# The second layer's attention of a decoder kernel, written as 384 equal slots

## The reference

```python
x = x + _L1_attn_ref(_layernorm(x, axis=-1), L1_attn_W_kqv, L1_attn_b_kqv, L1_attn_W_proj, L1_attn_b_proj, L1_attn_slopes)

def _L1_attn_ref(x, W_kqv, b_kqv, W_proj, b_proj, slopes):
    B, S, E, H = (2, 512, 256, 16)
    D = E // H
    kqv = x @ W_kqv + b_kqv
    k, q, v = jnp.split(kqv, 3, axis=-1)          # each reshaped to (b, s, H, D)
    attn = jnp.einsum('bqhd,bkhd->bhqk', q, k) * (1.0 / jnp.sqrt(jnp.float32(D)))
    bias = slopes[:, None, None] * jnp.tril(rel)  # rel = j - i
    bias = jnp.where(j > i, NEG_INF, bias)
    attn = jax.nn.softmax(attn + bias[None], axis=-1)
    y = jnp.einsum('bhqk,bkhd->bqhd', attn, v).reshape(b, s, e)
    return y @ W_proj + b_proj
```

## Time and profile before

| | |
|---|---|
| runs | 2440.0, 2426.59, 2440.98 us |
| profiled execution | 2440.0 us, span 2440.0 us |
| TensorE matmul busy | 2194.9 us (90%) |
| VectorE, ScalarE, GpSimd busy | 1186.6, 961.3, 641.1 us |
| mean granted TensorE clock | 0.945 |

### The profile page before, as it was taken

How to read it: one execution, slowest core, us unless ns; L and a number is a source line. 1 busy time by engine, 2 the same in 40 slices (tenths; PEclk the granted TensorE clock), 3 DMA queues, 4 the chain that set the end, 5 groups by cost and what they waited for, 6 DMA issues and landing times. The chain is left out here.

```text
span 2440.0 us, 41800 instructions
## 1 busy us (share of the span) xinstructions
PE 2194.9 (90%) x13788; PEld 1746.8 (72%) x13789; DVE 1186.6 (49%) x3470; ACT 961.3 (39%) x1878; POOL 641.1 (26%) x821
## 2 busy tenths in 40 slices
PE   6997888779999688888889879988999999999998
PEld 4664455568999445555555457778899999999998
DVE  4553788755334456666665345535322222222245
ACT  2222455333444344444444413320255555555411
POOL 1112667744401233333332211105400000000063
PEclk9997999889999789998999889989999999999999
DMA  9930000123222424442333010054211111111033
GB/s 321 386 109 1 1 1 33 46 72 117 70 69 84 97 54 88 88 88 49 83 80 70 2 56 4 3 193 148 88 31 34 34 34 34 32 32 34 26 110 101
DMA packets 151007, 183.45 MB, mean 75 GB/s; under 512 B 25490, under 2 KB 119250, under 8 KB 150738
## 3 DMA queue, kind: packets, MB, share of 16 engines
q1 hardware_dynamic: 136962, 146.51, 21.0%
q0 software_dynamic: 12288, 33.57, 4.4%
q10 hardware_dynamic: 1616, 1.57, 0.2%
HBM read 73.34 MB, written 74.19 MB: 60 GB/s over the span
## 5 line engine op out<-in xcount | busy, mean ns | idle before, releaser
L2462 ACT ACTIVATE a_prob<-a_st_ps 128x512 f32<-128x512 f32 (+1 forms) x384 | 197.6, 523 | 302.5 <-PE a_st_ps L2341 300.3
L2539 DVE CUSTOM_DVE_ANT_0 a_s_ps<-a_s_ps,a_causal 128x512 f32<-128x512 f32 (+3 forms) x512 | 241.0, 515 | 124.2 <-PE a_s_ps L2324 123.5
L1983 PE MATMUL e_up_ps<-e_xT,e_ring 128*128 128x128 f32 x2272 | 276.7, 275 | 0.0
L1983 PEld LDWEIGHTS e_up_ps<-e_xT,e_ring 128*128 128x128 f32 x2272 | 270.7, 192 | 3.7
L1935 POOL DMA_INDIRECT e_wgu<-slots_y,slot x64 | 61.2, 957 | 620.1 <-DMA slots_y<-e_y 575.6
L2013 ACT ACTIVATE e_ring<-e_wgu 128x512 f32 (+2 forms) x355 | 180.9, 531 | 75.6 <-PE e_up_ps L1983 73.9
L2324 PE MATMUL a_s_ps<-a_ks,rf_qs 68*128 68x512 f32 (+3 forms) x512 | 155.9, 373 | 60.7 <-DVE a_most L2539 47.5
L2018 ACT ACTIVATE e_hT<-e_up_ps 128x512 f32<-128x512 f32 x103 | 61.5, 597 | 371.9 <-PE e_y_ps L1993 364.4
L2341 PE MATMUL a_st_ps<-rf_qs,a_ks 128*128 128x512 f32 (+3 forms) x512 | 186.4, 415 | 15.7 <-DMA rf_qs<-a_m_lo 12.5
L2254 POOL TENSOR_SCALAR_AFFINE_SELECT a_prob<-a_prob 128x256 f32<-128x256 f32 x256 | 101.8, 423 | 367.2 <-ACT a_prob L2462 367.0
L1993 PE MATMUL e_y_ps<-e_wd,e_hT 128*128 x852 | 195.7, 379 | 0.0
(11 more groups left out here) (465 smaller groups left out, 4021.5 us busy)
## 6 DMA issues: line engine op xcount, KB each, us to landing
slots_x<-zero_row SPq DMA_DIRECT2D x4, 8448.0 KB, 50.6
e_xin<-slots_x SPq DMA_DIRECT2D x142, 128.0 KB, 2.0
rf_qs<-late_w SPq DMA_DIRECT2D x64, 256.0 KB, 5.8
a_ks<-late_w SPq DMA_DIRECT2D x64, 256.0 KB, 6.4
slots_x<-e_y SPq DMA_DIRECT2D x71, 128.0 KB, 1.7
slots_y<-e_y SPq DMA_DIRECT2D x71, 128.0 KB, 1.7
e_wgu<-in_L_ffn_wg SPq DMA_DIRECT2D x8, 688.0 KB, 9.7
e_wgu<-in_L_ffn_wu SPq DMA_DIRECT2D x8, 688.0 KB, 10.9
```

What stands on the lines that cost most here:

```text
L1983: last = pe.matmul(up_ps[:, j, bank, (first + n) * P:(first + n + 1) * P], weights, xT[:, j, k * P:(k + 1) * P], start=k == 0, stop=k == K ...
L2462: act.activation(prob[:, gr % 2, u // 3, (u % 3) * BANK:(u % 3) * BANK + cols], st_ps[:, u % 2, 0:cols], ACT.Exp).then_inc(exp_done, 1)
L2539: last = dve.tensor_tensor_reduce(s_ps[:, u % 2, off:off + cols], s_ps[:, u % 2, off:off + cols], causal[:, S - cols:], 1.0, -3.0e38, ALU. ...
```

## The change

The stage's 8 x 48 key units become slots 0 to 383, and each engine's program is one loop over the slots. A slot has one query unit (that of `slot + LEAD`, LEAD = 18) and one key unit; 18 query units run ahead of slot 0. Everything else has a fixed slot in the group (u) or in the sequence (`at`, 0 to 47). The row scaling of the next sequence moves from VectorE (`vector_rows`) to ScalarE (`scalar_rows`, one tile a slot), with its offsets on GpSimd; statistics and combines are done a tile at a time. The values of sequence 0 are projected ahead of slot 0.

The transfers of queries and keys go by groups of four heads: `spread_group`, 8 transfers of half the size, four times a sequence, each after the exponentials of the same group of the sequence before; for groups 0 and 1 of sequence 0 the four query transfers each go out from SyncE and the four key transfers from ScalarE. For this the weights and biases are ordered by (d, h) within 64 columns, which takes 8 GpSimd instructions of half the size instead of 4, and 8 bias loads instead of 4.

```diff
-    SCORES_AT = (1, 2, 1, 2, 1, 2, 1, 2, 0, 0, 0, 0)
-    TURN_AT, OUTPUTS_AT, KEPT_AT, TURN_OUTPUTS_AT = 9, 3, 7, 11
+    SEQ = G * UNITS
+    SLOTS = B * SEQ
+    LEAD = UNITS + 6
+    OUTPUTS_AT = {3: (0,), 4: (1,), 5: (2,), 6: (3,)}
+    TURN_MAXIMA_AT, HIGH_AT, LOW_AT, KEPT_AT, TURN_OUTPUTS_AT, NORMALISE_AT = 7, 8, 8, 9, 11, 1
+    VALUES_AT, KEEP_VALUES_AT = {0: 0, 1: 1, 2: 2, 4: 3}, {7: 0, 8: 1}
+    ROWS_AT, TURN_ROWS_AT, KEEP_ROWS_AT = {1: 0, 3: 1, 4: 2, 5: 3}, 10, 10
+    QK_AT, HIGH_QK_AT, LOW_QK_AT = {12: 0, 14: 1, 34: 2, 37: 3}, {13: 0, 15: 1, 35: 2, 38: 3}, {14: 0, 16: 1, 36: 2, 39: 3}
+    TURN_HEADS_AT, KEEP_HEADS_AT, PROJECT_AT, ADD_AT = 20, 20, {22: 0, 24: 1, 26: 2, 29: 3}, {26: 0, 31: 1}
+    COMBINE_AT, STATS_AT, WHOLE_STATS_AT = {17: 0, 18: 1, 28: 2, 29: 3}, {33: 0, 34: 1, 35: 2, 37: 3}, 40
...
+        def spread_part(eng, b, gr, part, which):
+            n = gr % (P // GP) * GP
+            dst, src = ((qs, (hi, lo)[part % 2][n:n + GP, 0]), (ks, (hi, lo)[part // 2][n:n + GP, 1]))[which]
+            eng.dma_start(dst[part:PARTS:4, gr * GH:(gr + 1) * GH, :].bitcast(F32), src.bitcast(F32)).then_inc(spread[gr], 16)
...
+            def spread_group(b, gr):
+                sp.wait_ge(qk_lo, 4 * b + 2 * (gr // 2) + 2)
+                after(sp, exp_done, UNITS * (G * (b - 1) + gr + 1))
+                for part in range(4):
+                    for which in range(2):
+                        spread_part(sp, b, gr, part, which)
...
+            sp.wait_ge(qk_lo, 2)
+            for gr in range(2):
+                for part in range(4):
+                    spread_part(sp, 0, gr, part, 0)
+            place_maxima(0)
+            spread_group(0, 2)
+            spread_group(0, 3)
+            for b in range(B):
+                if b:
+                    spread_group(b, 3)
                 for gr in range(G):
+                    if G * b + gr + 1 < B * G:
+                        place_maxima(G * b + gr + 1)
+                    if b + 1 < B and gr < G - 1:
+                        spread_group(b + 1, gr)
...
+            for slot in range(SLOTS):                       # TensorE
+                n, u = slot // UNITS, slot % UNITS
+                b, at = slot // SEQ, slot % SEQ
+                if slot + LEAD < SLOTS:
+                    score_by_query(slot + LEAD)
+                if u in OUTPUTS_AT and n:
+                    for t in OUTPUTS_AT[u]:
+                        outputs(n - 1, t)
+                if u == TURN_MAXIMA_AT and n + 1 < B * G:
+                    turn_maxima(n + 1)
+                if b and at in VALUES_AT:
+                    project_v(b, VALUES_AT[at])
+                if b + 1 < B:
+                    if at == TURN_ROWS_AT:
+                        norm.tensor(b + 1, free=[(v_kept, 2 * b + 2)])
+                    if at in QK_AT:
+                        project_qk(b + 1, QK_AT[at])
...
+                if u == TURN_OUTPUTS_AT and n:
+                    turn_outputs(n - 1)
+                score_by_key(slot)
...
+            for slot in range(SLOTS):                       # ScalarE
+                exponential(slot)
+                if u == HIGH_AT and n + 1 < B * G:
+                    high_maxima(n + 1)
...
+            for slot in range(SLOTS):                       # VectorE
+                if slot + LEAD < SLOTS:
+                    maximum(slot + LEAD)
+                if u == LOW_AT and n + 1 < B * G:
+                    low_maxima(n + 1)
+                if u == NORMALISE_AT and n >= 2:
+                    normalise(n - 2)
+                if b + 1 < B and at in LOW_QK_AT:
+                    low_qk(b + 1, LOW_QK_AT[at])
```

More of the change, by code:

```diff
@@ L103, in vector_stats, with vector_tile_stats, vector_whole_stats @@
     def vector_stats(self, b):
+        self.vector_tile_stats(b, range(TB))
+        self.vector_whole_stats(b)
+    def vector_tile_stats(self, b, tiles):
         v, x, st = self.nc.vector, self.g.x, self.stats
-        for t in range(TB):
+        for t in tiles:
             v.bn_stats(st[:, t, :], x[:, b * TB + t, :]).then_inc(self.stats_done, 1)
+    def vector_whole_stats(self, b):
+        v, st = self.nc.vector, self.stats
         v.wait_ge(self.stats_done, b * TB + TB)
@@ L147, in gpsimd_offset, with scalar_rows @@
         p.tensor_tensor(self.offset[:, :], self.minus[:, :], self.rstd[:, :], ALU.mult).then_inc(self.offset_done, 1)
-    def scalar_rows(self, b, free=(), buf=0):
+    def scalar_rows(self, b, free=(), buf=0, tiles=range(TB)):
         a = self.nc.scalar
@@ L2190, in l1_attention @@
         w_done, x_done = sem("w_done"), sem("x_done")
-        spread = [sem(f"spread{i}") for i in range(KT)]
+        spread = [sem(f"spread{i}") for i in range(G)]
         m_placed = [sem(f"m_placed{i}") for i in range(G)]
@@ L2271, in _ @@
             norm.gpsimd(1)
+            norm.gpsimd_offset(1)
             pool.wait_ge(x_done, 2)
-            def body(b, nxt, following):
+            for b in range(B):
+                following = b + 2 if b + 2 < B else None
                 for gr in range(G):
@@ L2290, in body @@
                     mask(b, gr, (3,))
-                    if gr == 3 and following is not None:
-                        norm.gpsimd(following)
-            over_sequences_ahead(body)
         @block.tensor
@@ L2343, in score_by_key, with outputs @@
                 last.then_inc(st_done, 1)
[L2345 to L2346 removed]
+            def outputs(n, t):
                 if t == 0:
@@ L2435, in _ @@
+            for t in range(TB):
+                outputs(B * G - 1, t)
+            turn_outputs(B * G - 1)
             pe.wait_ge(x_done, 2 * B)
-            turn_heads(B - 1, None)
+            turn_heads(B - 1)
             for t in range(TB):
@@ L2480, in _ @@
                 high_qk(0, i)
+            act.wait_ge(qk_lo, 2)
+            for gr in range(2):
+                for part in range(4):
+                    spread_part(act, 0, gr, part, 1)
+            for i in range(2):
+                keep_values(0, i)
             act.wait_ge(front.slopes_placed, SLOPES)
@@ L2516, in _ @@
-            over_sequences_ahead(body)
-            keep_outputs(B - 1, G - 1)
+            high_maxima(0)
+            for slot in range(SLOTS):
+                n, u = slot // UNITS, slot % UNITS
+                b, at = slot // SEQ, slot % SEQ
+                exponential(slot)
+                if u == HIGH_AT and n + 1 < B * G:
+                    high_maxima(n + 1)
+                if b and at in KEEP_VALUES_AT:
+                    keep_values(b, KEEP_VALUES_AT[at])
+                if b + 1 < B:
+                    if at in ROWS_AT:
+                        norm.scalar_rows(b + 1, tiles=(ROWS_AT[at],))
+                    if at == KEEP_ROWS_AT:
+                        norm.scalar(b + 1, free=[(v_done, 2 * b + 2)])
+                    if at in HIGH_QK_AT:
+                        high_qk(b + 1, HIGH_QK_AT[at])
+                if b and at == KEEP_HEADS_AT:
+                    keep_heads(b - 1)
+                if u == KEPT_AT and n:
+                    keep_outputs(n - 1)
@@ L2543, in low_maxima @@
-            def low_maxima(b, gr):
-                n = b * G + gr
+                wait_apart(dve, s_done, s + 1, (ready, READY))
+                for t, off in Q_UNITS[u % 3]:
+                    cols = (t + 1) * P
+                    last = dve.tensor_tensor_reduce(s_ps[:, u % 2, off:off + cols], s_ps[:, u % 2, off:off + cols], causal[:, S - cols:], 1.0,
+                                                    -3.0e38, ALU.add, ALU.max, most[:, n % 2, u // 3, t:t + 1])
+                last.then_inc(max_done, 1)
```

311 lines of the change are left out of this document (111 added, 200 removed).

## The result

The kernel after took 2373.5 us (median of four, 2371.4 to 2376.5), the kernel before beside it 2439.7 us (median): a ratio of 0.975 with a 95% interval of 0.9725 to 0.9776. The forecast was 2388 us in a range of 2342 to 2430, so 52 us of saving were forecast and 66 came. The profiled execution took 2376.5 us, with a span of 2374.7.

What follows compares the result with a forecast made beforehand. TensorE was the bound in name, with 11.8 of 65.8 us a clean sequence in waits and gaps; slots -38, clock -14, start -4, SyncE +4 and front 0 sum to -52 from 2440, 2388 us, range 2342 to 2430.

Steps and rivals of the forecast that it cites:

- Slots (-38): Attention slots: equal slots cut waits and gaps from 11.8 to 7.0 us, a sequence to 61.0; -38 us over eight.
- bare slots: 17 slots a sequence without other sizeable TensorE work, where two query-unit banks allow 0.69 us, not 0.60: 1.5 us waiting.
- bulges: Slots 36 to 38, smaller at 25 and 33, where VectorE's extra work holds TensorE: 1.5 us a sequence.
- slot-8 chain: Slot 8 of each group: VectorE waits for ScalarE's split of maxima, later maxima and TensorE queue; 0.5 a group, 2.0 us.
- Rival (b): In the slots, VectorE's extra work comes in series and holds TensorE; a sequence is 65.5 us, total 2427 us; chance 0.20.
- Columns and heads: Waits in the slots for turned columns kept one slot later (0.4 us) and for heads (0.6 us), per sequence.
- Maxima and SyncE (0.2 a sequence, +4): Placed maxima leave 0.2 us of wait a sequence; SyncE's spread issues ahead of them add 4 us over the stage.
- rival (c): SyncE's queue: maxima also wait for the spread's landing, 5.8 us late twice a sequence; 93 us, total 2481; chance 0.08.
- Clock (-14): Stage slots: of 28 us lost to stretches at 1.2 GHz, half come back with fewer waits; -14 us (0 to -28).
- Start (-4): Stage lead-in: half the bytes for the first group bring the first query unit 5 us earlier, 1 goes back; -4 us.
- Front (0, at most +2.4): Ahead of attention: four more GpSimd instructions and four more bias loads on SyncE cost 0, at most 2.4 us.
- Row scaling (0): Slots 1, 3, 4, 5: ScalarE takes 4 x 0.59 us a sequence at no cost, 17 us without cover.

Runs made afterwards that it cites:

- Between the halves: Kernel after, but SyncE places the maxima of groups 2 and 0 between the two halves of the spread beside them; 2423.2 us on a slower chip, ratio 0.968.
- eight-head kernel: Kernel after with equal slots, but transfers by eight heads and four bias loads as before; 2456.5 us, ratio 1.008 to the kernel before.
- both mends: Kernel after, but SyncE alone issues the first sequence's spreads, and maxima of groups 2 and 0 stand between spread halves; 2350.3 us, ratio 0.9649 to before.

## Why the prediction was right, and where not

**Slots (-38).** The largest term, and right in its cause: the even order shortens the sequence, and putting the old distribution back brings 64.6 to 65.4 us. Forecast 61.0, measured 59.3 to 59.6. It was too narrow in naming the wait. Idle time for row maxima in the slots fell from 44.0 us before to 19.5 already in the kernel with the old distribution, whose sequences are hardly shorter, and to 10.5 with the even order; there the even order gave more by ending waits for ScalarE.

Of the waits left, VectorE's were to be 5.0 us a sequence (bare slots 1.5, bulges 1.5, the slot-8 chain 2.0). The matmuls' idle time for VectorE is 1.4, in six places of 0.20 to 0.26. Four of them are the same place in each group, the 512-column query unit of slot 9. In three of these VectorE had itself just waited for TensorE, as here:

```profile
1106.65 0.57 DVE L2547 CUSTOM_DVE_ANT_0 a_s_ps<-a_s_ps,a_causal 128x384 f32<-128x384 f32 x1 [0.23 <-PE a_s_ps L2337]
...
1107.57 0.50 PE L2337 MATMUL a_s_ps<-a_ks,rf_qs 68*128 68x512 f32 x1 [0.23 <-DVE a_most L2547]
...
1108.40 0.28 DVE L2553 SCALAR_TENSOR_TENSOR a_m_lo<-a_m_ps,a_m_hi 16x128 fp32r<-16x128 f32 x1 [0.50 <-ACT a_m_hi L2462]
```

TensorE's wait ends before VectorE turns to the split, so this is not the slot-8 chain but the two banks in bare slots: 0.7 us of the 1.4. In the fourth such place VectorE is behind a combine, and in another behind the sum, 0.46 together: its bulges, though at slots 18 and 31 and not where the forecast had them. Only the sixth, 0.21 at 1094.10, stands behind a split. VectorE waited for ScalarE's high part once in this sequence, not once a group, and 7.1 us in all slots (49.9 before). So all three terms exist, and together they are a quarter of their forecast; the slot-8 chain, the largest, was nearly nothing. Rival (b), VectorE's extra work in series at 6 us a sequence, is refuted. Columns and heads cost 0.9 instead of 1.0, outputs nothing in this sequence instead of 0.8.

**Maxima and SyncE (0.2 a sequence, +4).** The place was right, the size was not. Together they forecast 1.6 + 4 = 5.6 us of idle time; it was 12.0, nine times, at 3.0 us the worst. The 2.4 us a sequence that the forecast set against its 0.2 were waits of weight loads; by that view 18.8 us became 16.4, and by the matmuls' idle time 12.5 became 12.0. The saving of 2.2 a sequence did not come. This is SyncE's queue in one such place:

```profile
1060.66 0.57 SPq L2208 DMA_DIRECT2D rf_qs<-late_w  x1
...
1065.13 0.60 SPq L2208 DMA_DIRECT2D a_ks<-late_w  x1
1065.78 0.60 SPq L2224 DMA_DIRECT2D rf_qs<-a_m_hi  x1
1066.42 0.59 SPq L2224 DMA_DIRECT2D rf_qs<-a_m_lo  x1
```

VectorE had the low part ready at 1064.9, while SyncE was still issuing the spread until 1065.7; TensorE lost 0.70 us. Issue for issue the sum was right (0.64 us), and it was this place that it named. It had no term for the landing. Here the key unit ran 3.0 us after the low part's issue (1069.42), and in the two worst places, idle for 3.0 us each, 3.8 and 4.3 us after it (issues at 877.79 and 944.17, units at 881.54 and 948.51), where the chain of before has 1.88 to the weights. In the last sequence, which has no spread, the kernel after has 1.88 too (1312.05 to 1313.93). So in seven of the eight places beside a spread 1.1 to 2.5 us passed beyond those 1.88, in the landing (in the eighth, idle 0.31 us, none did): the mechanism of rival (c), at a fraction of its price. That it is the spread's bytes is inferred from where it happens. Between the halves, with half as much ahead, turn and landing together leave 2.0 us in the whole stage.

**Clock (-14).** Slots at 0.92 lose about 2 x 0.08 x 546 = 87 us to the low level, at 0.95 about 48: 39 us less at 1.2 GHz, which are about half of that in time, 20. By the forecast's own measure it is less: six sequences (862.55 to 1229.23) take 366.7 us instead of 6 x 59.3 = 355.8, 11 over, 15 for eight, so 13 of 28 came back. The forecast's 14 was a choice of half, and it fell into that range. The Trainium skill, TensorE: Matmul & The Clock Gate, section "The HAM clock gate (the "warmup" mystery)", has activity release the full clock; the windows of the eight-head kernel agree, 0.55 behind a wait of 5.6 us and 1.00 afterwards. The full return that it was weighed for came in no run of the kernel after, and nearly in the one with both mends (0.98 in the slots).

**Start (-4).** Wrong: +2.8. The failed step is "ScalarE issues eight transfers (8 x 0.6, as SyncE's issues take), keeps values and writes four heads' rows first; that ends near 824". Two engines that issue together took 8.19 and 8.79 us for eight each, so ScalarE kept values 4.0 us later than 8 x 0.6 would have it (827.18 instead of 818.34 + 4.8), and TensorE's projections, which need the values' banks, stood 7.5 us behind them. The forecast said that the values lie in the wait; they had become the wait. With SyncE alone the first query unit comes 16.3 us behind the stage's first matmul, 4.9 earlier than before (21.2): the halved bytes did bring the 5 us expected of them. But from there to the first key unit it is 17.8 us instead of 15.1, so 2.7 went back where the forecast had 1, and the lead-in of 34.1 is only 2.2 under that of before. The Trainium skill, DMA: Bandwidth & Descriptors, section "Issuing engines are not separate DMA queues", leaves a second issuing engine only the time that issuing takes; here that was 1.5 us of 10.3, against 5.0 us of lead-in lost.

**Front (0, at most +2.4).** Wrong, at the far end and a little past it: +2.5 in the profiled run, 2.9 by the tiles' distances. Loads ahead did not cover it.

```profile
566.56 5.11 SPq L1407 DMA_DIRECT2D rf_bias<-in_L_attn_b_kqv  x8
```

It was 2.57 us for four before. The tile's load behind these came late (TensorE idle 0.85 us), and a window of 20 us at clock 0.91 instead of 1.00 followed, which cost more than the load itself.

**Row scaling (0).** Right: 59.7 against 59.3 us a sequence with it back on VectorE.

The forecast thus lay 14 us too high in spite of two small terms that missed the other way: the slots at equal clock, SyncE's term in them, gave 8 x (65.8 - 59.5) = 50 instead of 38 - 4 = 34. Start and front took 5.3 us where 4 were to be saved. Part of the closeness is therefore luck: misses of 16 us or more to one side met one of 9 to the other.

## What to carry to other kernels

When two kinds of unit share an engine and each has a ring of two banks, count what stands between two uses of a bank before counting busy shares: an order of 1,2,1,2,...,0,0 cost 5 to 6 us in 65 with no engine over 90% busy, and in the run that put the order back most of the idle time it brought stood behind ScalarE, not behind the engine that reads the crowded ring. An even order moves the limit to what must arrive in time, so transfers are cut to the size of the new step (by eight heads the same order was slower than before), and in a queue with a long batch the small urgent transfer goes between its halves. An engine that computes should not issue transfers ahead of something that another engine waits for. One profiled execution is one draw: here they lay up to 9 us from their medians.

## What the runs showed of the hardware

Sixteen issues took 10.3 us on SyncE alone (814.12 to 824.37, 0.64 each) and 8.8 us split over SyncE and ScalarE, 1.0 to 1.1 each on either (0.74 and 0.83 where ScalarE began 2 us later): the second issuing engine bought 15%, and stood still meanwhile (6.12 and 9.65 us in the rows above). An issue costs the same for half the rows: a bias load of 64 rows took 5.11 / 8 = 0.64 us, one of 128 rows 2.57 / 4 = 0.64. Issued in a row, transfers of 128 KB landed in 2.4 us (median) where those of 256 KB took 5.5 to 6.4; but the eight of 128 KB that ScalarE issued at the start, together with SyncE's eight, took 5.7. And behind 5.6 us of idle TensorE, 8 us of its work ran near 1.2 GHz.
